# Output bias of a token mixer added to the residual rows by GpSimd instead of by TensorE matmuls

## The reference

```python
x_prev = concatenate([zeros, x[:, :-1, :]], axis=1)
xk = x_prev + (x - x_prev) * tmk            # xv, xr in the same way
k = einsum('bth,oh->bto', xk, Wk) + bk      # v, r in the same way
wkv = _wkv_scan(k, v, time_decay, time_first)
rwkv = sigmoid(r) * wkv
out = einsum('bth,oh->bto', rwkv, Wo) + bo
x1 = _layernorm(x + out)
...
combine = one_hot(argmax(probs)) * gate
y = einsum('ne,neo->no', combine, einsum('nh,eoh->neo', x1, W) + b)
return _layernorm(x1 + y)
```

## Time and profile before

| what | us |
|---|---|
| median of 3 runs (lowest, highest) | 700.25 (700.14, 702.02) |
| the profiled execution | 702.84 |
| its span, first to last instruction | 701.0 |
| busy: PE, DVE, ACT, POOL | 600.3, 570.2, 374.9, 321.8 |
| start, until the first scan | 34.4 |
| the eight blocks and their tail | some 34 to 503 |
| sorting | some 503 to 540 |
| experts | some 540 to 701 |

### The profile page before, as it was taken

How to read it: one execution, slowest core, us unless ns; L and a number is a source line. 1 busy time by engine, 2 the same in 40 slices (tenths; PEclk the granted TensorE clock), 3 DMA queues, 4 the chain that set the end, 5 groups by cost and what they waited for, 6 DMA issues and landing times. The chain is left out here.

```text
span 701.0 us, 8827 instructions
## 1 busy us (share of the span) xinstructions
PE 600.3 (86%) x2521; PEld 447.4 (64%) x2522; DVE 570.2 (81%) x819; ACT 374.9 (53%) x656; POOL 321.8 (46%) x257
## 2 busy tenths in 40 slices
PE   0577779999999999999999999798613999999992
PEld 0365656676687677677677677464603777777871
DVE  7959899999999999999999996754697566676762
ACT  3355566477576476576477476442520355555542
POOL 4735444444445435435434431612257466666641
PEclk9889999999999999999999999988655799999996
DMA  8030010041032031031031041053420344444430
GB/s 302 2 120 1 0 61 0 2 150 31 0 122 60 0 120 58 2 107 60 13 106 60 16 165 60 16 168 131 134 106 16 93 141 134 142 140 137 139 119 5
DMA packets 26863, 56.80 MB, mean 81 GB/s; under 512 B 3832, under 2 KB 3832, under 8 KB 26836
## 3 DMA queue, kind: packets, MB, share of 16 engines
q1 hardware_dynamic: 20596, 37.85, 16.3%
q0 software_dynamic: 6240, 18.62, 8.3%
HBM read 39.64 MB, written 18.61 MB: 83 GB/s over the span
## 5 line engine op out<-in xcount | busy, mean ns | idle before, releaser
L916 POOL TENSOR_TENSOR mixed<-unsplit,mixed 128x1024 fp32r<-128x1024 f32 x44 | 104.5, 2394 | 133.7 <-ACT mixed L637 133.7
L434 PE MATMUL kb<-mixed,w_kvr 128*128 128x512 f32 x384 | 98.8, 408 | 24.4 <-DVE mixed L1289 16.7
L434 PE MATMUL vb<-mixed,w_kvr 128*128 128x512 f32 x384 | 102.1, 417 | 14.9 <-DVE evn L1104 9.2
L610 PE MATMUL y_ps<-w_e,xgT 128*128 x468 | 114.8, 394 | 0.0
L434 PE MATMUL rb<-mixed,w_kvr 128*128 128x512 f32 x384 | 102.9, 418 | 9.0 <-DVE ee L1118 7.7
L434 PEld LDWEIGHTS kb<-mixed,w_kvr 128*128 128x128 f32 x384 | 74.2, 197 | 42.7 <-issue 16.3
L452 PE MATMUL y_ps<-w_o,rw 128*128 128x512 f32 x224 | 100.8, 593 | 0.0
L610 PEld LDWEIGHTS y_ps<-w_e,xgT 128*128 128x128 f32 x468 | 88.7, 190 | 18.1
L434 PEld LDWEIGHTS vb<-mixed,w_kvr 128*128 128x128 f32 x384 | 74.4, 198 | 36.1 <-DVE evn L1104 12.0
L434 PEld LDWEIGHTS rb<-mixed,w_kvr 128*128 128x128 f32 x384 | 74.1, 195 | 31.7 <-DVE ee L1118 9.0
L1055 DVE SCALAR_TENSOR_TENSOR unsplit<-diff,vec,xb 128x512 f32<-128x512 f32 x96 | 74.2, 834 | 8.1 <-PE kb L434 6.0
(11 more groups left out here) (178 smaller groups left out, 1024.4 us busy)
## 6 DMA issues: line engine op xcount, KB each, us to landing
rows<-x SPq DMA_DIRECT2D x32, 256.0 KB, 2.7
x_rows<-rows SPq DMA_DIRECT2D x32, 256.0 KB, 2.1
we_raw<-w_experts SPq DMA_DIRECT2D x8, 1024.0 KB, 6.0
xb<-xT SPq DMA_DIRECT2D x4, 1026.0 KB, 5.3
xb<-xT SPq DMA_DIRECT2D x3, 1024.0 KB, 5.1
w_raw<-w_square SPq DMA_DIRECT2D x2, 1024.0 KB, 9.7
xb<-xT SPq DMA_DIRECT2D x2, 512.0 KB, 5.1
w_raw<-w_square SPq DMA_DIRECT2D x2, 512.0 KB, 6.8
```

The source lines that it names most:

```text
L434: mm = pe.matmul(bank, w_kvr[:, m, a, h, o:o + P], mixed[:, m, bb, h, :], start=(k == 0), stop=(k == 3 * CH - 1))
L610: mm = pe.matmul(y_ps[:, parity, :], xgT[:, third, a, c, :], w_e[:, bass.ds(e, 1), bb, c, :].rearrange("p u o -> p (u o)"), start=False, s ...
L916: pool.tensor_tensor(mixed[:, m, LO, 2 * hp:2 * hp + 2, :], unsplit[:, m, LO, 2 * hp:2 * hp + 2, :], mixed[:, m, HI, 2 * hp:2 * hp + 2, :] ...
```

## The change

`bo` is no longer split and no longer goes through TensorE. SP loads it once, broadcast to all 128 partitions, into a new tile `bo_all` (float32). POOL adds it to each residual row tile as soon as that is loaded (`bias_rows_of`, a 128x512 addition with both inputs in SBUF), and DVE's `add_rows` waits for that addition (`row_biased`) in place of the load. The bias matmul of each of the 32 output tiles is gone; the first `w_o` matmul starts the bank. With `bo2` go one memset, and two of the four small transfers.

```diff
-            sp.dma_start(b_raw[EXPERTS:EXPERTS + 1, :], bo).then_inc(bo_loaded, 16)
...
+            sp.dma_start(bo_all[:], bo.rearrange("u o -> (u o)").partition_broadcast(P)).then_inc(bo_loaded, 16)
...
-            def bias_out(bank):
-                pe.matmul(bank, ones[:], bo2[:], start=True, stop=False)
...
-                bias_out(y_ps[:, j % 2, :])
                 for c in range(CH):
                     mm = pe.matmul(y_ps[:, j % 2, :], rw[:, half, c, j * P:(j + 1) * P], w_o[:, c, :],
-                                   start=False, stop=(c == CH - 1))
+                                   start=(c == 0), stop=(c == CH - 1))
...
+            def bias_rows_of(n, j):
+                pool.wait_ge(row_loaded[j], n * 16 + 16)
+                pool.tensor_tensor(rows[:, j], rows[:, j], bo_all[:], ALU.add).then_inc(row_biased, 1)
...
                 else:
                     expert_lo(pool, 0)
+                if s.prev:
+                    bias_rows_of(i - 1, 0)
+                    bias_rows_of(i - 1, 1)
                 leave(i, 2)
 
                 if not s.last:
                     mix_lo(i + 1, V, 0)
                     mix_lo(i + 1, V, 1)
-                else:
+                if s.prev:
+                    bias_rows_of(i - 1, 2)
+                    bias_rows_of(i - 1, 3)
+                if s.last:
                     expert_lo(pool, 1)
                 leave(i, 3)
...
+            pool.wait_ge(bo_loaded, 16)
             walk(pool, step, pool.Fori)
-            for q in (2, 3, 5):
+            expert_lo(pool, 2)
+            for j in range(TPB):
+                bias_rows_of(BLOCKS - 1, j)
+            for q in (3, 5):
                 expert_lo(pool, q)
...
-                dve.wait_ge(row_loaded[j], n * 16 + 16)
+                dve.wait_ge(row_biased, n * TPB + (j + 1))
                 dve.wait_ge(y_filled, n * TPB + (j + 1))
```

More of the change, by code:

```diff
@@ L142, in build @@
         bias_rows = place("bias_rows", [P, H], F32R)
-        bo2 = place("bo2", [P, H], F32R)
+        bo_all = place("bo_all", [P, H], F32)
         ident = place("ident", [P, P], F32)
@@ L180, in build @@
         raw_at = base + 7 * mat
-        b_raw = place("b_raw", [EXPERTS + 1, H], F32, at=raw_at)
-        b_split = place("b_split", [EXPERTS + 1, 2, H], F32R, at=raw_at + 4 * H)
+        b_raw = place("b_raw", [EXPERTS, H], F32, at=raw_at)
+        b_split = place("b_split", [EXPERTS, 2, H], F32R, at=raw_at + 4 * H)
         zero_row = place("zero_row", [1, H], F32, at=raw_at + 4 * 3 * H)
@@ L282, in build @@
         row_loaded = [sem(f"row_loaded{j}") for j in range(TPB)]
+        row_biased = sem("row_biased")
         row_stored = [sem(f"row_stored{j}") for j in range(TPB)]
@@ L377, in _ @@
                 sp.dma_start(w_raw[K][:, half], w_v[K][:, half]).then_inc(w_k_loaded[hp], 16)
-            sp.dma_start(b_raw[0:EXPERTS, :], b_experts).then_inc(b_loaded, 16)
-            sp.dma_start(b_raw[EXPERTS:EXPERTS + 1, :], bo).then_inc(bo_loaded, 16)
+            sp.dma_start(b_raw[:], b_experts).then_inc(b_loaded, 16)
             for n in (V, R):
@@ L389, in _ @@
                 sp.dma_start(bias_rows[s * EXPERTS:(s + 1) * EXPERTS, :].bitcast(F32),
-                             b_split[0:EXPERTS, s, :].bitcast(F32)).then_inc(bias_moved, 16)
-                sp.dma_start(bo2[s:s + 1, :].bitcast(F32),
-                             b_split[EXPERTS:EXPERTS + 1, s, :].bitcast(F32)).then_inc(bias_moved, 16)
+                             b_split[:, s, :].bitcast(F32)).then_inc(bias_moved, 16)
             walk(sp, step, sp.Fori)
@@ L447, in project_out @@
                     pe.wait_ge(w_loaded[O], 16)
-                    pe.wait_ge(bias_moved, 64)
-                    pe.wait_ge(route_const, 1)
-                bias_out(y_ps[:, j % 2, :])
                 for c in range(CH):
                     mm = pe.matmul(y_ps[:, j % 2, :], rw[:, half, c, j * P:(j + 1) * P], w_o[:, c, :],
-                                   start=False, stop=(c == CH - 1))
+                                   start=(c == 0), stop=(c == CH - 1))
                 mm.then_inc(y_filled, 1)
@@ L528, in out_pair @@
             def out_pair(j, pair):
-                if pair == 0:
-                    bias_out(y_banks[j])
                 for c in range(2 * pair, 2 * pair + 2):
                     mm = pe.matmul(y_banks[j], rw[:, HALVES - 1, c, j * P:(j + 1) * P], w_o[:, c, :],
-                                   start=False, stop=(c == CH - 1))
+                                   start=(c == 0), stop=(c == CH - 1))
                 if pair == 1:
@@ L613, in expert @@
                 mm.then_inc(expert_filled, 1)
+            pe.wait_ge(bias_moved, 32)
             pe.wait_ge(tiles_ready, 1)
@@ L823, in _ @@
             act.wait_ge(b_loaded, 16)
-            act.wait_ge(bo_loaded, 16)
             act.activation(b_split[:, HI], b_raw[:], ACT.Copy).then_inc(b_hi, 1)
@@ L1255, in _ @@
             cs[-1].then_inc(consts_set, 1)
-            dve.memset(bias_rows[:].bitcast(F32), 0.0)
-            dve.memset(bo2[:].bitcast(F32), 0.0).then_inc(bias_zero, 1)
+            dve.memset(bias_rows[:].bitcast(F32), 0.0).then_inc(bias_zero, 1)
             dve.wait_ge(consts_set, 1)
@@ L1301, in _ @@
             mix_matrix(0, R, 1)
-            dve.wait_ge(bias_moved, 64)
+            dve.wait_ge(bias_moved, 32)
             dve.wait_ge(zero_stored, 16)
```

## The result

The changed kernel takes 704.75 us (median of 8 runs, 704.02 to 706.2), the kernel before, run beside it, 701.55 (700.14 to 703.87). The ratio is 1.0045 with a 95% interval of 1.0029 to 1.0062: 3.2 us slower. The forecast was +3.4, or 703.7 from the median of 700.25 that the first three runs had given.

A forecast was written before the change was run, and what follows sets the result against it. In the steady part PE and DVE were both taken as nearly full, with DVE alone setting the pace after the change. 7.8 + 0.3 - 4.5 - 0.2 = +3.4 us on 700.25 gave 703.7, forecast range 702 to 707, overall 698.5 to 708.

The forecast's parts named there:

- The additions hold L1125 and L1131: Blocks 1 to 6: two POOL additions delay L926 and L928, which hold these DVE instructions; 1.3 us a block, 7.8 in all.
- The second pair: Blocks 1 to 6: a block's other two additions delay `leave` to where DVE's small L1153 stands; 0.05 us a block, 0.3 in all.
- The waits of 4.5 us: Blocks 2 to 6: DVE's waits behind bias matmuls, for the last r and last output tile, plus one for v, all go.
- The 0.5 us without a named releaser: Steady blocks: one DVE wait, for the next v, counted within the 4.5 us that would go.
- The last block and its tail: Last block and behind the loop: 0.8 and 0.4 us given back, 1.0 lost; together -0.2, 1.2 either way.
- The start: Before DVE's first scan at 34.4 us: dropping the `bo` split, two small transfers and a memset counts for nothing.
- DVE going on first: Rival, blocks 1 to 6: L1131 runs ahead of waiting L928, so only L1125's 0.4 to 0.8 us are lost; 699.4 us, chance 0.18.
- nothing held: Rival: no stall at L1125 in the blocks, and the 4.5 us of waits go; 695.5 us, chance 0.10.
- The clock: Rival: PE idles more and its clock falls at the k of chunk 3, 1.6 us in three blocks; 708.5 us, chance 0.12.
- the idle time of some 3.4 us behind block 1: Behind block 1: one PE idle time of some 3.4 us, which DVE doesn't wait for.

The follow-up runs named there:

- e1: Changed kernel with POOL's additions for tiles 0 and 1 moved behind `leave` of chunk 0 in every block; 700.53 us, ratio 0.9982 to the kernel before.
- e5: Changed kernel with those two additions behind `leave` of chunk 0 in blocks 1 to 6 only, last block as in the changed kernel; 697.77 us, ratio 0.9935 to before.
- e8: Changed kernel with a zero-adding bias matmul of the old 128-row form put back ahead of each output tile; 704.16 us, ratio 1.0019 to before.
- e2: Kernel before without its 32 bias matmuls and with no additions, output bias left out; 696.47 us, ratio 0.9924 to before.

## Why the prediction was right, step by step

- **The additions hold L1125 and L1131.** Right in kind and nearly in size. An addition took 1.27 us and not 1.15 (2.54 for two), L1125 1.58 (1.6 to 2.0 forecast), L1131 2.00 (2.04). In all 1.1 to 1.2 us a block against 1.3, 6.9 against 7.8, shown to come from the place by e1 and e5. The Trainium skill says the same in "SBUF — State Buffer", section "Who interferes with whom": two SBUF operands on DVE suffice. This trace agrees, with 1.58 and 2.00 us for instructions of 1.22. The two-port modes alone, which are what the Trainium skill's "Advanced Engine Details and Errata", section "Mode Summary", names, would have left both at 1.22.
- **The second pair: 0.3 us.** Nothing in the blocks; the small L1153 (now L1158) took 0.15 or 0.16 us throughout.
- **The waits of 4.5 us go.** Not quite these. The 0.5 us without a named releaser stayed (0.5 after, too; why isn't shown). The ten others, 4.0 us of idle time, went, and by the lag each gave back some 0.1 more than its idle time: 5.0 in all, 4.5 of it up to the r of block 6. So 6.9 - 4.5 is the 2.4 measured there, but the equality with the forecast's 4.5 is chance. The credit was wrongly given as well. The sum sets the 4.5 us against the matmuls taken away, and only a parenthesis says that the delay alone would end most of them. e8 shows that it ends all of those behind the output matmuls. So beside the holds the matmuls' removal brought nothing in blocks 1 to 6, and the additions' whole cost there is 2.4 us. Alone the removal brings 4.2 (e2), beside additions that hold nothing 4.1 (e5). The sum came out near all the same, because either way the waits are gone and DVE's own work, holds included, sets the pace.
- **The last block and its tail: -0.2, with 1.2 either way.** The steps held: L1125 no longer behind the split, the small L1153 (now L1158) held by the first addition for block 7, 1.06 us against 1.0. From the rb of chunk 1 to the end of the first quotient it took 20.27 us against 20.94, 0.7 less (0.8 forecast). From there to the next L1125 it gave back 0.7 where 0.4 was forecast for the bias matmul, and 0.7 more up to 487 us, mostly on output matmuls (y_ps 5.77 us before, 5.08 after) that also differ between the two traces of before (5.77 and 5.29); so the trace has -1.0 behind the last wait of block 6 in place of -0.2. Missed was the tie: with the addition first, that place costs 4.4 us more. The range of 1.2 us for the tail was too small.
- **The start: nothing.** Both traces of after were 1.5 us late there. The trace of before isn't, its repetition is, so the change is not needed for it. The rows of all fourteen traces fall into two groups: where PE idled 0.98 to 1.31 us ahead of the first r projection, it took 3.0 to 3.1 us and the trace isn't late (five traces); where PE idled 1.85 to 2.01, it took 4.2 to 4.6 and the trace is 1.4 to 2.1 us late (nine). The longer idle time follows a quicker first projection, 4.4 to 5.0 us against 5.49. Why that one is quicker isn't shown, and whether the change makes it likelier stays open: of the traces with additions 8 of 10 are late, of those without 1 of 4.
- **The rivals.** DVE going on first would have left L1131 at 1.23, nothing held both; neither was so. The clock didn't fall at the k of chunk 3 (3.04 us after 0.84 of idle, and PE idled at most 1.0 there); the idle time of some 3.4 us behind block 1 didn't come either, the longest there was 1.6.

The total of +3.4 against +3.2 is thus closer than its parts: +2.4 in place of 3.6 for the blocks, +1.5 in place of nothing for the start, and a rest that varies from run to run by more than the difference. The mechanism was right; that the number came so near is partly luck.

## What to carry to other kernels

Two engines that both look full make a maximum, not a sum: what is taken from one is worth only the waits that the other still has, and a delay uses these up first. Before work is moved to GpSimd, look at which VectorE instructions with two SBUF operands it will stand beside; the same additions made the blocks 6.5 us longer in one place than in another. And look at the long GpSimd instructions that are already there: three waits in front of them brought over three times what the change was about.

## What the runs showed of the hardware beyond that

- A held instruction costs by what it waits for, not by its own size: 128x1 elements stood 4.14 us behind a 128x2048 split.
- Which of two instructions that start within 0.01 us of each other goes first differed between two executions of one program (451.34 and 451.35, then 451.31 twice), and that decided 4.4 us.
- A bias matmul on 64 rows was dearer than one on 128: 0.42 us to the next start against 0.23 or 0.31, 0.11 more for the four behind it and 0.1 to 0.2 more for what stood ahead of it, some 0.4 a tile. Why isn't shown.
- After the same 3.92 us of idle the same twelve matmuls took 5.49 us in one execution and 4.60 in another (granted clock 0.50, that is 1.2 GHz, to the end in the first; 0.78 on average over the last 1.8 us in the second).
